# Four-layer recurrent kernel: the first feed-forward stage's results, gathered by token afterwards or scattered to token order while the tiles run

## The reference

```python
weights = _router(x, expert_embeddings)            # softmax over the two best of 8 experts
ones = (weights > 0)
cap_ones = where(cumsum(ones, axis=0) <= expert_capacity, ones, 0.0)   # 1024 rows an expert
vals, idx = top_k((weights * cap_ones).T, expert_capacity)
tokens = x_flat[idx.reshape(-1)].reshape(E, expert_capacity, hidden)
out = einsum(relu(einsum(tokens, first_linear)), second_linear) * vals[:, :, None]
final = zeros((n_tokens, hidden)).at[index].add(out)
```

## Time and profile before

| | us |
|---|---|
| median of three runs (6416.99, 6424.23, 6426.39) | 6424.23 |
| profiled execution, its own time | 6420.27 |
| its span from first to last instruction | 6418.5 |
| causal attention, layer 0 | 0 to 1115 |
| experts of layer 0: loads until PE starts | 1116.7 to 1129.7 |
| experts of layer 0: tiles | 1129.7 to 1196.6 |
| experts of layer 0: gather and combine | 1199.8 to 1372.8 |
| next phase starts | 1377.3 |

### The profile page before, as it was taken

How to read it: one execution, slowest core, us unless ns; L and a number is a source line. 1 busy time by engine, 2 the same in 40 slices (tenths; PEclk the granted TensorE clock), 3 DMA queues, 4 the chain that set the end, 5 groups by cost and what they waited for, 6 DMA issues and landing times. The chain is left out here.

```text
span 6418.5 us, 101900 instructions
## 1 busy us (share of the span) xinstructions
PE 5656.5 (88%) x33881; PEld 2996.4 (47%) x33881; DVE 4334.3 (68%) x9917; ACT 3828.7 (60%) x8010; POOL 2970.8 (46%) x2847
## 2 busy tenths in 40 slices
PE   8999998439999799999999889999999999896643
PEld 3444443312222466666666634444444444464443
DVE  4555553246666677777787678888888888685624
ACT  2444444126666577777777667777777777674322
POOL 1225234356777667666666433232332323154355
PEclk9999998769999899999999999999999999999876
DMA  1000001430000111111111110000000000031324
GB/s 38 8 11 30 14 17 34 122 81 11 14 13 8 54 33 32 30 33 39 40 46 44 35 29 12 19 10 12 19 12 19 10 12 17 17 89 44 107 68 122
DMA packets 348505, 225.99 MB, mean 35 GB/s; under 512 B 30290, under 2 KB 324946, under 8 KB 347730
## 3 DMA queue, kind: packets, MB, share of 16 engines
q1 hardware_dynamic: 328624, 183.83, 10.9%
q0 software_dynamic: 12288, 25.19, 1.5%
q10 hardware_dynamic: 7074, 10.46, 0.5%
HBM read 104.24 MB, written 68.55 MB: 27 GB/s over the span
## 5 line engine op out<-in xcount | busy, mean ns | idle before, releaser
L3816 PE MATMUL a_scores_ps<-a_kT,a_q_mixed 128*128 128x512 f32 x2048 | 1046.3, 593 | 3.7 <-ACT a_probs L3626 3.1
L3826 PE MATMUL a_acc_ps<-a_probsT,a_v_post 128*128 128x512 f32 x2048 | 1042.8, 592 | 0.4 <-DVE a_probsT L3719 0.4
L3626 ACT ACTIVATE a_probs<-a_scores_ps,a_neg_max 128x512 f32<-128x512 f32 x1024 | 703.0, 687 | 427.2 <-DVE a_neg_max L3709 417.9
L3709 DVE TENSOR_REDUCE a_neg_max<-a_scores_ps 128x1 f32<-128x512 f32 x1024 | 693.4, 677 | 202.4 <-PE a_scores_ps L3816 197.9
L3719 DVE STREAM_TRANSPOSE a_probsT<-a_probs 128x512 f32<-128x512 f32 x1024 | 715.4, 699 | 135.7 <-PE a_acc_ps L3826 112.2
L3631 ACT ACTIVATE a_probs<-a_probs,a_inv_sum 128x512 f32<-128x512 f32 x1024 | 727.8, 711 | 0.8 <-DVE a_inv_sum L3714 0.8
L2949 DVE TENSOR_REDUCE a_neg_max<-a_pair_ps 128x2 f32<-128x1024 f32 (+3 forms) x512 | 417.6, 824 | 353.8 <-PE a_pair_ps L3045 349.1
L2753 ACT ACTIVATE a_probsT<-a_pair_ps 128x1024 f32<-128x1024 f32 (+3 forms) x512 | 359.4, 704 | 483.8 <-PE a_pair_ps L3058 482.3
L3826 PEld LDWEIGHTS a_acc_ps<-a_probsT,a_v_post 128*128 128x128 f32 x2048 | 389.0, 190 | 490.9 <-issue 488.8
L3816 PEld LDWEIGHTS a_scores_ps<-a_kT,a_q_mixed 128*128 128x128 f32 x2048 | 384.4, 190 | 476.6 <-issue 438.9
L3572 POOL TENSOR_TENSOR a_q_mixed<-a_qT,a_pre 128x512 f32<-128x512 f32 x248 | 250.3, 1041 | 759.8 <-PE a_scores_ps L3816 759.8
(11 more groups left out here) (416 smaller groups left out, 11852.0 us busy)
## 6 DMA issues: line engine op xcount, KB each, us to landing
f_v_even<-f_v_odd SPq DMA_DIRECT2D x224, 130.0 KB, 2.3
attention_out<-a_s_out SPq DMA_DIRECT2D x64, 256.0 KB, 2.3
f_gs<-attention_out SPq DMA_DIRECT2D x64, 256.0 KB, 4.4
a_v<-a_v_rows SPq DMA_DIRECT2D x256, 64.0 KB, 2.1
a_x<-x_after SPq DMA_DIRECT2D x48, 256.0 KB
f_x<-x_after SPq DMA_DIRECT2D x48, 256.0 KB, 5.5
f_gx<-x_after SPq DMA_DIRECT2D x48, 256.0 KB, 3.3
x_after<-f_gout SPq DMA_DIRECT2D x32, 256.0 KB, 2.4
```

The costliest lines, as they stand in the source:

```text
L3626: act.activation(probs[:, n % NPR, :], scores_ps[n % NS][:], ACT.Exp, bias=neg_max[:, n % NS:n % NS + 1], scale=1.0, accum_out=row_sum[:, ...
L3709: dve.tensor_reduce(neg_max[:, n % NS:n % NS + 1], scores_ps[n % NS][:], AX.X, ALU.max, negate=True).then_inc(max_ready, 1)
L3816: pe.matmul(scores_ps[n % NS][:], q_mixed[:, g % 2, i].rearrange("f a q -> f (a q)"), kT[:, par, :], start=True, stop=True).then_inc(score ...
L3826: pe.matmul(acc_ps[par][:], v_post[:, g, i, :], probsT[:, g % NT, i, :], start=(p == 0), stop=(p == U - 1)).then_inc(products_done, 1)
```

## The change

In the attention phase each row of `xn_all` grows from 128 to 132 floats (528 bytes): both gates, the rank of the first pick's expert, and the token's own row number ("home"). They are scattered with the row. SP no longer stores `slots` and `gates` and no longer zeroes `x_sorted`; it copies a filler table from DRAM to the 16 groups (rows nobody claims are sent home to spare rows), and in bodies 0 to 15 it zeroes two sequences' worth of `y_rows`, a table of 2 x 8192 token rows and 8192 spare ones. One load (`home`) joins the 15 at the start, as the eighth on ACT's queue. DVE's routing chain has 33 operations: one more before `picks_ready`, which comes at step 8 where it came at step 7, and two fewer after it.

In the expert phase DVE works out, for groups 0 to 3 and later 4 to 15, each sorted row's gate and its home row (first picks to rows 0 to 8191, second picks to the next 8192). `keep_y` multiplies by the gate where it copied, into one of 16 buffers, and POOL scatters the 128-row tiles to `y_rows` right behind it (64 indirect DMAs). SP loads x and attention of all 16 sequences early, then, when all scatters have landed, both picks' rows of a sequence with plain loads into 4 buffers. DVE adds the two; POOL multiplies the attention by the sum; DVE does the last two operations, two sequences behind.

```diff
-    GROUPS = 17
+    GROUPS = 16
+    WIDE = D + 4
+    GATES, FIRST, HOME = D, D + 2, D + 3
-        self.slots = dram("slots", (P, 2, batches * NC), mybir.dt.int32)
-        self.gates = dram("gates", (P, 2, batches * NC))
+        self.x_sorted = dram("x_sorted", ((self.GROUPS + 1 + 2 * batches) * T, self.WIDE))
+        self.y_rows = dram("y_rows", (2 * NB * T + self.GROUPS * T, D))
...
-    PICK_OPS, WEIGH_OPS, PLACE_OPS = 12, 5, 17
+    PICK_OPS, WEIGH_OPS, PLACE_OPS = 12, 6, 15
-        xn = sb("xn_all", [P, batches, NC, D])
+        xn = sb("xn_all", [P, batches, NC, routes.WIDE])
+                 (home[:], dram["L0f_home"][:, 0:batches * NC])]
+            for g in range(routes.GROUPS):
+                sp.dma_start(routes.x_groups[g], fill_groups[g]).then_inc(filled, 16)
             sp.wait_ge(zeros_ready, 1)
-            for g in range(routes.GROUPS - 1):
-                sp.dma_start(routes.x_groups[g], zeros[:]).then_inc(zeroed, 16)
...
-                if group_at(n - 1) is not None:
-                    store_routes(group_at(n - 1))
+                if 0 <= n <= LAST:
+                    for k in range(2):
+                        sp.dma_start(routes.y_batches[k, n], zeros[:]).then_inc(zeroed, 16)
...
+                if i == 17:
+                    op = dve.tensor_copy(tail[:, :, routes.GATES:routes.GATES + 2].rearrange("p n k -> p k n"), weight[:, :, 0:N])
...
-                if i == 31:
-                    op = dve.scalar_tensor_tensor(gates[:, :, r0:r1], taken_sum[:, :, 0:N], 0.0, weights_of, ALU.is_lt,
-                                                  ALU.mult)
-                    op = dve.tensor_scalar(slots[:, :, r0:r1], taken_sum[:, :, 0:N], dump[:, 0:1], None, ALU.add)
...
-                    if s == 7:
+                    if s == 2 + WEIGH_OPS:
                         dve.wait_ge(route_chain, g * ALL_OPS + PICK_OPS + WEIGH_OPS)
                         dve.sem_inc(picks_ready, 1)
+            dve.tensor_copy(xn[:, :, :, routes.HOME], home[:].rearrange("p (b c) -> p b c", c=NC))
```

The expert phase:

```diff
-            for g in range(GROUPS):
-                sp.wait_ge(y_kept, g + 1)
-                sp.dma_start(routes.y_groups[g], y_tiles[:, g % 4]).then_inc(y_stored[g % 4], 16)
+            for b in range(batches):
+                sp.dma_start(gx[:, b], x_rows[b]).then_inc(gate_loaded, 16)
+                sp.dma_start(gs[:, b], s_rows[b]).then_inc(gate_loaded, 16)
+            def load_y(b):
+                if b >= 4:
+                    sp.wait_ge(scaled, b - 3)
+                    sp.wait_ge(sigmoid_ready, b - 3)
+                for k in range(K):
+                    sp.dma_start(y[:, b % 4, k], routes.y_batches[k, b]).then_inc(y_loaded[b % 4], 16)
+            sp.wait_ge(rows_scattered, 16 * GROUPS * NC)
+            for b in range(min(4, batches)):
+                load_y(b)
             for b in range(batches):
                 sp.wait_ge(out_ready, b + 1)
                 sp.dma_start(out_rows[b], out[:, b % 2]).then_inc(out_stored[b % 2], 16)
-                if b + 2 < batches:
-                    load_gate(b + 2)
+                if b + 4 < batches:
+                    load_y(b + 4)
...
-            for b in range(batches):
-                for pick in range(2):
-                    for c in range(NC):
-                        row = b * NC + c
-                        pool.indirect_dma_start(y[:, b % 4, pick, c, :], None, routes.y_sorted, ...)
+            for g in range(GROUPS):
+                pool.wait_ge(homes_ready, 1 if g < 4 else 2)
+                pool.wait_ge(y_kept, g + 1)
+                for t in range(NC):
+                    n = g * NC + t
+                    pool.indirect_dma_start(routes.y_rows, bass.IndirectOffsetOnAxis(ap=homes[:, n:n + 1], axis=0),
+                                            y_tiles[:, g, t, :], None).then_inc(rows_scattered, 16)
+            pool.wait_ge(gate_loaded, 32 * batches)
+            for b in range(batches):
+                pool.wait_ge(y_summed, b + 1)
+                pool.tensor_tensor(gs[:, b], gs[:, b], y[:, b % 4, 0], ALU.mult).then_inc(scaled, 1)
...
+            act.dma_start(expert[:], dram["L0f_expert"]).then_inc(weights, 16)
...
-                dve.tensor_copy(y_tiles[:, g % 4].rearrange("p c d -> p (c d)"), y_ps[g % 2][:]).then_inc(y_kept, 1)
+                dve.tensor_tensor(y_tiles[:, g], y_ps[g % 2][:].rearrange("p (c d) -> p c d", c=NC), weights_of,
+                                  ALU.mult).then_inc(y_kept, 1)
+            def homes_of(g0, g1):
+                for g in range(g0, g1):
+                    dve.wait_ge(loaded[g], 16)
+                ...
+                if g in (0, 4):
+                    homes_of(*((0, 4) if g == 0 else (4, GROUPS)))
+                    dve.sem_inc(homes_ready, 1)
...
-            for b in range(batches + 1):
+            for b in range(batches + 2):
                 if b < batches:
-                    combine(b)
-                if b >= 1:
-                    finish(b - 1)
+                    add_picks(b)
+                if b >= 2:
+                    finish(b - 2)
```

More of the change, by code:

```diff
@@ L2578, in causal_attention_phase @@
         spare = sb("spare", [P, 2, batches * NC])
-        gates, slots = sb("gates", [P, 2, batches * NC]), sb("slots", [P, 2, batches * NC], mybir.dt.int32)
+        home = sb("home", [P, batches * NC])
         to_rows = sb("to_rows", [P, 2, batches * NC], mybir.dt.int32)
@@ L2809, in normalise @@
                 for c in range(NC):
-                    last = dve.tensor_scalar(xn[:, b.at, c, :], rows.x[:, c, :], rows.moments[:, c, 0:1],
+                    last = dve.tensor_scalar(xn[:, b.at, c, 0:D], rows.x[:, c, :], rows.moments[:, c, 0:1],
                                              rows.rstd[:, c:c + 1], ALU.subtract, ALU.mult)
@@ L3087, in turn_rows @@
                 for c in range(NC):
-                    last = pe.transpose(misc[:, c * P:(c + 1) * P], xn[:, b.at, c, :], ident[:])
+                    last = pe.transpose(misc[:, c * P:(c + 1) * P], xn[:, b.at, c, 0:D], ident[:])
                 last.then_inc(rows.xn_turned, 1)
@@ L3237, in dispatched_experts_phase @@
         w1, w2 = sb("w1", [D, E * K, P]), sb("w2", [P, E * K, D])
-        x = sb("x", [P, GROUPS, NC, D])
+        x = sb("x", [P, GROUPS, NC, routes.WIDE])
         xT = sb("xT", [D, 2, T])
         hidden = sb("hidden", [P, 2, K, T])
-        y_tiles = sb("y_tiles", [P, 4, NC, D])
-        zeros = sb("zeros", [P, NC, D])
-        slots = sb("slots", [P, 2, batches * NC], mybir.dt.int32)
-        gates = sb("gates", [P, 2, batches * NC])
+        y_tiles = sb("y_tiles", [P, GROUPS, NC, D])
+        expert = sb("expert", [P, GROUPS * NC])
+        other, gate1, gate2 = (sb(name, [P, GROUPS * NC]) for name in ("other", "gate1", "gate2"))
+        homes = sb("homes", [P, GROUPS * NC], mybir.dt.int32)
         y = sb("y", [P, 4, 2, NC, D])
-        gx, gs = sb("gx", [P, 2, NC, D]), sb("gs", [P, 2, NC, D])
+        gx, gs = sb("gx", [P, batches, NC, D]), sb("gs", [P, batches, NC, D])
         gate, out = sb("gate", [P, 2, NC, D]), sb("out", [P, 2, NC, D])
@@ L3258, in dispatched_experts_phase @@
         y_done, y_kept = sem("y_done"), sem("y_kept")
[L3259 to L3261 removed]
+        y_loaded = [sem(f"y_loaded{n}") for n in range(4)]
+        gate_loaded, scaled = sem("gate_loaded"), sem("scaled")
         y_summed, sigmoid_ready, out_ready = sem("y_summed"), sem("sigmoid_ready"), sem("out_ready")
@@ L3401, in turn @@
                 for t in range(NC):
-                    last = pe.transpose(turn_ps[g % 2][:, t * P:(t + 1) * P], x[:, g, t, :], ident[:])
+                    last = pe.transpose(turn_ps[g % 2][:, t * P:(t + 1) * P], x[:, g, t, 0:D], ident[:])
                 last.then_inc(turned, 1)
@@ L3897, in constants @@
     out["L0f_spare"] = np.broadcast_to(apart, (P, 2, NB * NC)).astype(np.float32).copy()
+    out["L0f_home"] = (128.0 * np.arange(NB * NC)[None, :] + i).astype(np.float32)
+    slot = np.arange(Routes.DUMP)
+    fill = np.zeros((Routes.DUMP, Routes.WIDE), np.float32)
+    fill[:, Routes.FIRST], fill[:, Routes.HOME] = 8 - slot // Routes.CAPACITY, 2 * NB * T + slot
+    out["L0f_fill"] = fill
+    out["L0f_expert"] = np.broadcast_to(8.0 - np.arange(NB * NC) // 8, (P, NB * NC)).astype(np.float32).copy()
     out["L3f_rank"] = np.broadcast_to(8.0 - np.arange(8), (P, 8)).astype(np.float32).copy()
```

128 lines of the change are left out of this document (51 added, 77 removed).

## The result

The changed kernel takes 6338.01 us in the median of four runs (6335.77 to 6340.41), the kernel before 6425.27 (four runs, 6416.99 to 6426.39): a ratio of 0.9869, 95% interval 0.9855 to 0.9882. Forecast were 6341 and 6318 to 6370. The profiled execution took 6335.77 us with a span of 6334.0, that of before 6420.27 and 6418.5: 84.5 us less of span.

What follows compares the result with a forecast made beforehand. POOL's serial chain of 128 gathers, 164 us behind the expert tiles, was taken as the bound. 85.4 us saved less 0.5, 1 and 1 is 82.9: 6420.3 becomes 6337.4, median 4 above, 6341; range 6318 to 6370.

Steps and rivals of the forecast that it cites:

- The chain: Expert phase: 128 gathers behind the tiles become 64 scatters beside them plus a combining loop on plain loads; 85.4 us saved.
- the additions: Costs added: start +0.5, later `picks_ready` +1, loads before the tiles +1; other added work 0.
- The ring: Combining loop: four buffers of loads pace it, 7.4 us for two sequences, finish(15) at 1287.4.
- The ring that is slower: Rival, combining loop: bursts and POOL-DVE hindrance give 5.2 us a sequence, +21, 6362; chance 0.15 together with slower scatters.
- The ring that doesn't bind: Rival, combining loop: loads land in 2.8 us or less, DVE alone paces it at 2.2 a sequence, -21, 6320; chance 0.12.
- a floor: Combining loop: if POOL and DVE excluded each other, at least 3.35 us a sequence, ending near 6336.
- No overlap: Rival, expert phase: POOL held until the tiles end, 64 scatters start at 1197, +54, 6395; chance 0.04.
- Wide rows: Rival, attention phase: 528-byte rows slow POOL's scatters; doubled, +82, 6423; chance 0.03 in part, 0.03 in full.
- PE's first transpose: Kernel start: it waits for the last small load, and the new one is issued 0.45 us later, +0.5.
- The loads before the tiles: Expert phase start: wider rows and expert table add 0.3 us, 4.6 if wide rows move at half speed; taken as +1.
- `picks_ready` at step 8: Attention phase: signal behind a maximum delays PE's count about 0.5 us for each of three groups; taken as +1.
- DRAM to DRAM copies: Kernel start: filler copies replace zero stores; even at twice the time nothing waits for them until 533, cost 0.

Runs made afterwards that it cites:

- loads first: Changed kernel with SP issuing the next loads of y ahead of the wait for the finished sequence and its store: 6338.88 us, on another chip 6328.03.
- gate late: Changed kernel with x and attention loaded a sequence at a time in the combining loop, not during the tiles: 6356.55 us, ratio 0.9894.

## Why the prediction was right

**The chain went as reckoned.** Forecast: scatters at 1.267 from 1140.1, the last one through at 1221.2, landed at 1223.4, first sum at 1227. Measured: 1.265, from 1141.7, the last one started at 1221.4, the first load of y issued at 1223.64, first sum at 1227.44. These times hold the additions too, so the chain is compared from the end of the first kept result. From there (1140.12) to the end of the combining (1372.76) the kernel before takes 232.6 us; the changed one, from 1140.91 to 1286.98 + 0.69 = 1287.67, takes 146.8, for a forecast 147.3: 85.9 us saved, forecast 85.4. The additions had moved the first kept result by 0.8, forecast 2.5. The phase's exit, which I left as it was, is 1.0 us shorter (3.50 for 4.54). Together that is 86.1 us at the next phase's start, forecast 82.9.

**The ring was right in kind and in sum, wrong in its parts.** I put a turn of two sequences at 7.4 us: landing 4.2 and 2.2 of DVE behind it, the finish 1.38 of that. Measured, from the store at 1235.68 to that at 1280.76 with six turns: 7.51. Inside it the loads landed in 3.5 us in the median, not 4.2, and the finish took 2.3, not 1.38, since its addition ran beside POOL's product and took 1.63 for 0.69. Two errors of 0.7 and 0.9 that nearly cancel: the sum is right by luck to that extent. A second piece of luck is in its ends. The ring began late: the second finish ended at 1238.53, not at 1235.6, since the third sum started at 1232.47, not at my 1231, and each finish was longer. And the last of its seven turns took 3.7 us (1284.01 to 1287.67), since the last two sequences wait for no load; I had given it 7.4. Late by 2.9 and shorter by 2.7, these cancel too. Putting the product on DVE shows the finish's part: the addition is back to 0.69, and the loop gains 1.9 to 2.4 us, not the 6 to 7 that seven turns of 0.95 would be, because a fourth DVE operation takes its place in the turn.

**The rivals.** The ring that is slower, from engines that hinder each other: the hindrance was there, but at 0.9 us of a turn's 7.5 and offset by quicker loads, where the rival had 3 us more a turn. The ring that doesn't bind: excluded for this kernel by the 9.8 us for which DVE waits for loads in the ring, and loads first shows what it would have brought, 11 us on the stretch. I had given 3.35 us a sequence as a floor if DVE and POOL excluded each other; loads first ran at 2.87. DVE's operations in a row start about 0.60 apart, not 0.692, and three of those with the product's 1.27 make 3.1; the last 0.2 are not explained. What lengthened some gathers to 1.28 no run here tests. No overlap: 54.8 us, forecast 54. Wide rows: no price on POOL, at 528 and at 640 bytes.

**The additions were smaller than their sum of 2.5.** PE's first transpose starts at 9.62, 9.53 before: +0.09 for +0.5. I had charged the last queue entry for a whole issue, but the load that was waited for then had been landing behind others anyway (that last part is argued, not shown). The loads before the tiles: from the first issue, 1118.74, to PE at 1131.20 are 12.46 us; before, 1116.66 to 1129.69, 13.03. The other executions with 528-byte rows take 12.45 to 13.39, so all that can be said is that my +1 doesn't stand out of what executions differ by. The Trainium skill says that a descriptor that doesn't start on 256 bytes fetches from the boundary below and pays beats for it (DMA: Bandwidth & Descriptors, How a descriptor splits into AXI transactions). My estimate of 1.2 us by it took 20.25 beats a row; with whole beats it is 20.5, and 1.3 us. No such price shows here.

`picks_ready` at step 8: PE's counts start at 492.99 and 882.25, before at 492.74 and 882.01, both 0.24 later, and that much was there at an attention store before the first of them (410.65 for 410.42). The attention store at 1056.84, behind the third count, is 0.24 later as well. So the step cost nothing, for my +1. The end of the attention phase came later by 2.1 in the profiled execution (1115.2 for 1113.1), but by 1.0 and 0.9 in the two unedited ones since, so half of it belongs to the execution. The rest I can't split: the kernel before has one profile only.

After the next phase begins, the changed kernel takes 6334.0 - 1291.17 = 5042.8 us, the one before 5041.2, the two repeats 5043.4 and 5046.8. The change touches nothing there; that is the run's own scatter, and the reason why 86.1 us saved up to that point appear as 84.5. The median then lies 2.2 us above the profiled execution where I had put 4, which brings 6341 to the measured 6338.

## What to carry to other kernels

A serial chain of small indirect DMAs on POOL is worth its whole length once it stands beside work of PE, and it costs the same there: 55 of the 87 us here. Halving their number counts only for what still sticks out. In a ring, issue the next load ahead of the store that waits for the slowest engine: the edit of two moved lines was worth more than moving an operation between engines. And before an operation goes to POOL to relieve DVE, look at what DVE does in that moment: with two inputs in SBUF on both sides they take turns, and DVE alone was quicker with all four.

## What the runs showed of the hardware

**DVE and POOL take turns.** In each turn of the loop above, DVE's addition starts 0.56 us after POOL's product and ends at 1246.20, 0.55 after the product's end at 1245.65; the product itself, which starts while DVE's L3385 is under way, is longer by 0.37. Both are, within 0.16 us, as one would have it if the later of the two stood still until the other is done. The Trainium skill says that a DVE instruction with two SBUF inputs contends with a GpSimd instruction that reads SBUF, and that the shared ports are an exclusive lock (SBUF — State Buffer, Who interferes with whom), and the trace agrees. POOL's scatters, by contrast, kept 0.96 us beside DVE's work in the tiles, whose 128x512 operations take at least one input from PSUM.

**DRAM to DRAM copies in 528-byte rows landed late, and it cost nothing.** The 16 filler copies landed in 10.0 us in the median, the zero stores they replace in 3.6; at 640-byte rows it was 6.0. From 5 to 35 us the DMA engines' busy share was 1.10 where it was 0.61, for 173 GB/s against 168. Nothing waited for it, as forecast.

**Stalls in the tiles on one chip.** On the first chip of the experiments, three kernels with scatters beside the tiles lost 28 to 35 us in them, counted from the first kept result to the last (13 to 15 of it at the last scatter, the rest was slack), the waits being put down to a remote signal:

```profile
DVE f_y_tiles L3351 <- remote: 36.6, 5, 10.6
ACT f_xT L3318 <- remote: 20.9, 3, 8.9
```

These are of loads first, from 1140 to 1240 us. In such a stretch PE issues single instructions 0.7 us apart, each of 0.27 to 0.47:

```profile
1185.07 0.27 PE L3426 MATMUL f_y_ps<-f_w,f_hidden 128*128 128x128 f32 x1 [0.91 <-issue]
...
1185.77 0.27 PE L3426 MATMUL f_y_ps<-f_w,f_hidden 128*128 128x128 f32 x1 [0.43 <-issue]
...
1186.48 0.27 PE L3404 MATMUL f_turn_ps<-f_ident,f_x 128*128 128x128 f32 x1 [0.45 <-issue]
```

PE's clock didn't begin it: in loads first it was granted 1.00 from 1140 to 1170 us, where PE was already busy only 23.98 of 30 us (30.00 in the changed kernel), and fell to 0.83 and 0.79 in the next two stretches of 30. Nor did the 8 MB of loads beside the tiles: gate late has none of them there and stalled as much. With the scatters after the tiles, on that chip, there was no stall. Two of the three kernels ran again elsewhere without any, as did every other kernel with scatters beside its tiles, and 10.9 and 17.5 us faster. So they go with the chip or the time, together with the scatters, and not with the product or loads first edits; gate late ran only there. What delays PE's signals there stays open, and the unedited kernel was not run on that chip; if it lost the same 13 to 15 us there, the gain would be an estimated 72 to 74 us instead of 87.
